# A two-layer correlation convolution on one core: the order in which products fill a PSUM bank, and group statistics one slot ahead

## The reference

```python
def _gn(v, G=32, eps=1e-05):                       # over 16 channels x 1024 pixels
    m, s = mean(g), var(g)
    return (g - m) / sqrt(s + eps)

def conv(feature, conv_w, conv_b):                 # K = 5, per batch
    fn = feature / maximum(norm over channels, 1e-12)
    fp = pad(fn, 2 pixels on each side)
    corr = stack([sum over channels of fp[:, :, r:h + r, cc:w + cc] * fn
                  for cc in range(5) for r in range(5)])
    cat = concatenate([feature, corr], axis=1)     # 512 + 25 channels
    return relu(einsum('oc,bchw->bohw', conv_w, cat) + conv_b)

x = x + conv(_gn(x), w0, b0)
x = x + conv(_gn(x), w1, b1)
```

## Time and profile before

| | |
|---|---|
| median of three runs | 539.26 us (538.2 to 539.94) |
| the profiled execution | 537.76 us, of which the span of all instructions is 536.0 us |
| busy share of the span | PE 88%, DVE 69%, ACT 53%, POOL 24% |
| chain that ended last, by engine | PE 54%, DVE 21%, ACT 8%, issue 6%, DMA 6% |
| channel matmuls (L565) | 1536, 518.6 us of overlapping busy time |
| products (L489, L502) | 4096 matmuls, 171.2 us of overlapping busy time |
| ACT tiles: L655, L662 | 64 of 1526 ns, 52 of 1315 ns |

### The profile page before, as it was taken

The page is one execution under the profiler, slowest core; times in us unless marked ns, Lnnn a source line. Parts: engine busy times, 40 slices in busy tenths (PEclk is TensorE's granted clock), DMA queues, the critical chain, the costliest instruction groups (busy, mean ns, idle before and its releaser), DMA issues.

```text
span 536.0 us, 13926 instructions
## 1 busy us (share of the span) xinstructions
PE 471.2 (88%) x5896; PEld 260.5 (49%) x5896; DVE 370.6 (69%) x869; ACT 285.5 (53%) x338; POOL 126.1 (24%) x179
## 2 busy tenths in 40 slices
PE   0548499499968999999899899999999999999996
PEld 0535255264634646464545546464646454454442
DVE  6789796769778396876859495877868694723322
ACT  1542355566393574839375574749393846623222
POOL 3542410131510313131201313131312112140400
PEclk9989799699998999999999999999999999999999
DMA  8261613440400445357474663131222325363432
GB/s 305 98 223 55 206 42 92 130 120 19 111 25 20 101 176 166 92 179 240 159 231 162 183 245 95 45 93 47 71 67 51 80 70 149 106 190 106 128 126 113
DMA packets 35013, 65.88 MB, mean 123 GB/s; under 512 B 12780, under 2 KB 22052, under 8 KB 34950
## 3 DMA queue, kind: packets, MB, share of 16 engines
q1 hardware_dynamic: 25158, 56.07, 31.4%
q0 software_dynamic: 9792, 8.92, 7.4%
HBM read 33.54 MB, written 28.87 MB: 116 GB/s over the span
## 4 chain that ended last, share of the span: by engine, by line
PE 54%; DVE 21%; ACT 8%; issue 6%; DMA 6%; POOL 2%; SPq 2%; DVEq 0%; ACTq 0%
PE conv_ps L565 38%; PE gram_ps L489 6%; DVE stats L779 5%; PE gram_ps L502 4%; DVE operands L826 4%; PE conv_ps L574 4%; ACT v L662 4%; DMA vol<-corr_h 4%; ACT operands L655 3%; DVE xs L909 2%; DVE operands L832 2%; POOL vol L300 1%; PE turn_ps L555 1%; POOL v L429 1%; DVE wmax L881 1%
## 5 line engine op out<-in xcount | busy, mean ns | idle before, releaser
L565 PE MATMUL conv_ps<-operands,wh 128*128 128x512 f16 x1024 | 324.0, 381 | 1.0 <-DVE wl L897 1.0
L565 PE MATMUL conv_ps<-operands,wl 128*128 128x512 f16 x512 | 194.6, 380 | 0.0
L565 PEld LDWEIGHTS conv_ps<-operands,wh 128*128 128x128 f16 x1024 | 101.4, 99 | 120.0 <-issue 1.9
L689 ACT ACTIVATE act_out<-conv_ps,bias,wdown 128x512 f32<-128x512 f32 x128 | 95.8, 770 | 117.8 <-DVE xs L909 66.7
L826 DVE TENSOR_TENSOR operands<-v,operands 128x1024 f16<-128x1024 f32 x64 | 81.8, 1279 | 61.7 <-ACT v L662 55.4
L909 DVE TENSOR_TENSOR xs<-xs,act_out 128x512 f32<-128x512 f32 x128 | 86.2, 685 | 34.2 <-ACT act_out L689 34.1
L655 ACT ACTIVATE operands<-xs,affine 128x1024 f16<-128x1024 f32 x64 | 97.1, 1526 | 20.7 <-DVE affine L819 20.7
L489 PE MATMUL gram_ps<-operands 128*32 128x108 f16 (+1 forms) x2048 | 85.4, 291 | 13.7 <-DVE operands L832 6.6
L489 PEld LDWEIGHTS gram_ps<-operands 128*32 128x32 f16 x2048 | 79.0, 139 | 21.8 <-issue 20.3
L502 PE MATMUL gram_ps<-operands 128*32 128x72 f16 (+1 forms) x2048 | 85.8, 271 | 2.4 <-issue 2.4
L779 DVE BATCH_NORM_STATS2 stats<-xs 128x6 f32<-128x512 f32 x128 | 79.9, 681 | 2.4 <-DMA xs<-in_x_dram 2.4
(11 more groups left out here) (70 smaller groups left out, 220.5 us busy)
## 6 DMA issues: line engine op xcount, KB each, us to landing
xs<-in_x_dram SPq DMA_DIRECT2D x32, 512.0 KB, 6.4
out_dram<-xs SPq DMA_DIRECT2D x32, 512.0 KB, 3.4
band_dram<-band SPq DMA_DIRECT2D x128, 60.0 KB, 2.7
skew<-band_dram SPq DMA_DIRECT2D x32, 222.5 KB, 3.1
vol<-corr_h POOLq DMA_DIRECT2D x48, 50.0 KB, 2.7
rows_dram<-rows SPq DMA_DIRECT2D x32, 65.8 KB
rows_dram<-rows SPq DMA_DIRECT2D x32, 63.3 KB
mirror<-rows_dram POOLq DMA_DIRECT2D x14, 110.9 KB, 2.5
```

The source lines that it names most:

```text
L565: pe.matmul(conv_ps[:, g % 4, :], w[:, l, t, m * P:(m + 1) * P], opnd[:, u % RING, part, t, n * HALF:(n + 1) * HALF], start=(t == 0 and w ...
L689: act.activation(in_rows(act_out[:, g % 2, :]), by_rows(conv_ps[:, g % 4, :]), ACT.Relu, bias=bias[:, l, m:m + 1], scale=wdown[:, l, m:m + ...
```

## The change

- A window of products lies in gram_ps in the order (y x e) in place of (y e x), the order in which the moving pixels pass. ACT's band copy puts it back into (y e x) and so reads PSUM in steps of two values.
- `norm_tile`, `exact_tile` and POOL's exact tiles write in order and read xs alternating between two image rows (x in steps of 4 bytes, the rows 128 bytes apart). Before they read in order and wrote every second value.
- For the units that `early` names (5 to 8 and 12 to 15) statistics, average and scale are moved ahead. In slot k, for unit k + 2: `stats_tile` 0 and 1 at the head of DVE, 2 at j = 3, 3 at j = 4, `stats_done` at j = 5, `average` on PE at j = 6 behind the turn, `deviations` and `unit_affine` at j = 7. In the next slot ACT does tile 0 of that unit ahead of the band copies. The other units (`late`) keep their places.

```diff
+        def in_bands(a):
+            return a.rearrange("p (y x e) -> p y x e", e=TROWS, x=WI)
+        def by_bands(a):
+            return a.rearrange("p (y e x) -> p y x e", e=TROWS, x=WI)
...
+        AVERAGE_AT, AFFINE_AT = 6, 7
+        def early(u):
+            return valid(u) and u > STEADY + 1 and (unit_layer(u) == 1 or unit_batch(u) < XRING)
+        def late(u):
+            return valid(u) and not early(u)
...
-                    pool.tensor_scalar(by_rows(v[:, t % 2, :]), in_rows(xs[:, ring_slot(unit_batch(u)), t, :]),
+                    pool.tensor_scalar(in_bands(v[:, t % 2, :]), by_bands(xs[:, ring_slot(unit_batch(u)), t, :]),
...
-                at = at.rearrange("p (y e x) -> p y x e", x=WCOLS, e=TROWS)
+                at = at.rearrange("p (y x e) -> p y x e", x=WCOLS, e=TROWS)
...
-                    if valid(k + 1):
+                    if late(k + 1):
                         average(k + 1)
...
+                    if j == AVERAGE_AT and early(k + 2):
+                        average(k + 2)
...
-                act.activation(by_rows(opnd[:, u % RING, 0, t, :]), in_rows(xs[:, ring_slot(unit_batch(u)), t, :]),
+                act.activation(in_bands(opnd[:, u % RING, 0, t, :]), by_bands(xs[:, ring_slot(unit_batch(u)), t, :]),
...
-                act.activation(by_rows(v[:, t % 2, :]), in_rows(xs[:, ring_slot(unit_batch(u)), t, :]), ACT.Identity,
+                act.activation(in_bands(v[:, t % 2, :]), by_bands(xs[:, ring_slot(unit_batch(u)), t, :]), ACT.Identity,
...
-                act.activation(band[:, n, :], gram_ps[:, n, 0:PITCH], ACT.Copy).then_inc(band_sb, 1)
+                act.activation(band[:, n, :].rearrange("p (y e x) -> p y e x", e=TROWS, x=WCOLS),
+                               gram_ps[:, n, 0:PITCH].rearrange("p (y x e) -> p y e x", e=TROWS, x=WCOLS),
+                               ACT.Copy).then_inc(band_sb, 1)
...
             for k in range(STEADY, SLOTS):
+                if early(k + 1):
+                    norm_tile(k + 1, 0)
+                    exact_tile(k + 1, 0)
...
+                    if j == AFFINE_AT and early(k + 2):
+                        deviations(k + 2)
...
-                if valid(k + 1):
+                if late(k + 1):
                     unit_affine(k + 1)
+                if early(k + 2):
+                    stats_tile(k + 2, 0)
+                    stats_tile(k + 2, 1)
...
-                        for t in {4: (0, 1), 5: (2,), 6: (3,)}.get(j, ()):
+                        for t in ({3: (2,), 4: (3,)} if early(k + 2) else {4: (0, 1), 5: (2,), 6: (3,)}).get(j, ()):
                             stats_tile(k + 2, t)
-                        if j == 7:
+                        if j == (5 if early(k + 2) else 7):
                             stats_done(k + 2)
+                    if j == AFFINE_AT and early(k + 2):
+                        unit_affine(k + 2)
```

More of the change, by code:

```diff
@@ L746, in _ @@
                     band_out_of_psum(k, 1)
-                    if valid(k + 1):
+                    if late(k + 1):
                         deviations(k + 1)
-                    if valid(k + 1):
                         norm_tile(k + 1, 0)
                         exact_tile(k + 1, 0)
+                    if valid(k + 1):
                         norm_tile(k + 1, 1)
```

## The result

The changed kernel takes 557.34 us (median of 4 runs, 554.95 to 562.25) against 538.73 before; the ratio is 1.037 [1.033, 1.041]. Ratios stand with their 95% interval and can differ a little from the quotient of the two medians (here 1.035). The change is slower by 3.7%, where 9% was forecast. The time lies inside the forecast range of 527 to 604, but by errors in opposite directions: one term was far too dear, and others stood at nothing. The profiled run took 558.75 us, span 557.0, clock 0.938 over the span where it was 0.973.

The account below looks back on a forecast made before the run. PE was taken as the bound, with one us of margin before the turn. Dearer ACT tiles and early averages, less the products' gain, summed to +48 us on the profiled 537.8: 586, or 587 on the median; range 527 to 604.

Parts of the forecast that it names:

- ACT's tiles: Norm and exact tiles on ACT: reading in jumps adds 0.79 us a tile, the contiguous f16 write saves 0.1.
- T: ACT's time per norm or exact tile: 1.285 us before, forecast 1.98, lower end 1.2 if jumps cost nothing.
- t: When ACT's last tile ends in a slot: 19.3 us with next unit early, 24.2 late, at T = 1.98.
- the rival: The faster rival: ACT's read with jumps costs nothing, T = 1.2, and products gain; 530 us, chance 0.39.
- the skew: SP's second skew issue lands late, so DVE's neighbour scaling waits; at T = 1.2 it sets 14.2 us.
- the five slots between early units: Slots 5, 6, 11 to 13: 34.4 us each, +27.6 in all; 29.3 each, +2.3, at T = 1.2.
- start and end: Kernel's start (units 0 to 2) +4 us and end -2 by the products; together -4 at T = 1.2.
- The moved steps: Early average waits for DVE's 8.9 us behind ACT's last tile; such a slot lasts at least t + 15.1 us.
- The products and the clock: PE's products: side-by-side PSUM writes save 1.0 us with a code stall, 2.3 without; granted clock 1.00 in these stretches.
- Slots 7 and 14, 8 and 9: Slots 7 and 14: PE's own work, 27.9 us each, -3.6; slots 8 and 9: 33.0 each, +4.9.
- the likeliest case: ACT pays for its read with jumps, T = 1.98: 587 us, range 566 to 604, chance 0.54.
- the first rival: ACT's read with jumps costs nothing, T = 1.2, and products gain: 530 us, 525 to 540, chance 0.39.

Follow-up runs that it names:

- e_only: Kernel before with only the early statistics, averages and scales moved; windows and ACT's tiles as before: 557.39 us, ratio 1.0356.
- done4: Changed kernel with the early aggregates one place earlier on DVE, ahead of the addition of j = 4: 548.55 us, ratio 1.0213 to the kernel before.
- avg7: Changed kernel with the early average one place later on PE, behind group 6: 531.31 us, ratio 0.9878 to the kernel before.
- p_only: Kernel before with only the new window order in gram_ps and its band copy: 534.54 us, ratio 0.9945.
- p_split: Kernel before with the new window order and band copy, second bank's products behind the first channel group, average between: 555.54 us, ratio 1.0338.

## Why the prediction was wrong, step by step

**ACT's tiles: the mechanism exists, the size was wrong.** The term was +0.79 us a tile, T = 1.98, and with it t = 19.3 and 24.2. Measured: +0.14 us on the f32 tile, T = 1.36. A price taken from another engine (DVE, two operands, jumps of 80 bytes) was made the forecast for want of a nearer row; the kernel had a nearer hint, that ACT wrote in 8-byte steps at 1.30 ns an element, and I gave it only to the rival. On the f32 tile the sign agrees with the rule on SBUF's lines in the Trainium skill (SBUF — State Buffer, "Specifications (TRN2)"), by which each crossing to a new line pays: 1315 to 1458 ns, 11%, net of what the new write order does. The f16 tile went the other way, from 1526 to 1461 ns.

Three slips in the sum are small: 513 - 362 ns over 200 elements is 0.755 ns and not 0.77; t at T = 1.2 is 13.1 and not 14.0, which the skew's 14.2 hides; slots 3 and 4 at T = 1.2 add up to 65.4 and not 66.4. And the old PSUM step was 20 values, a window's row in the code (`WCOLS`, of which 18 are filled), and not 18.

Put T = 1.36 into the prediction's own sums (t = 14.4 and 19.3): the five slots between early units 29.5, slot 10 34.4, slots 8 and 9 at 28.4, slots 3 and 4 66.9, start and end at -2: 534 us for the profiled run. The measured one is 558.75. So without this error the forecast would have been 0.7% faster, of the wrong sign, and off by 25 us. What follows is about these 25.

**The moved steps: the chain was right, its list of waits was short by one.** For slot 10 the 8.9 us from ACT's end to the average came out to the tenth, and slots 11 to 13 have 8.9 to 9.0. The step "this behind low_tile 3, which waits for ACT's last tile" left something out: three additions were counted in DVE's chain by their duration, 0.6 us each, but the third belongs to the next unit's group 0, whose volume PE holds back to the place right before the turn. The rows of before could show it: `HOLD` in the code, and ACT's rectifications that wait for PE at this place. In slots 4, 5, 6, 11 and 13 this addition is what releases the average (e_only has it too, done4 moves it, avg7 covers it). Its worth is small, though: in slots 5 and 6 the average starts 9.2 us behind ACT's end, only in slot 4 much later, 11.3. And a wait like the measured 1.67 us stands in the prediction's own sums at T = 1.36: 29.5 for a slot less 27.9 of PE's own work is 1.6.

That the five slots between early units took 155.6 us and not 5 x 29.5 has other reasons, which the prediction had at nothing. In slots 5 and 6 ACT's last tile ends at 17.1 and 16.5 and not at 14.4, behind products with code waits of 2.69 and 2.16 us and a clock of half behind them: ACT's tiles share its program with rectifications that wait for PE. In slots 11 and 12 the clock falls behind the wait at the average, and from the average to the slot's end it takes 7.6 us where 6.1 were allowed and 5.95 are taken at full clock (slots 5, 6 and 13).

**The products and the clock: pace right, net gain wrong, clock taken as 1.00.** The step fell to 80 ns as forecast. The forecast kept 1.0 us of a product with a code wait and 2.3 of one without, 21 us in all; p_only measured some 3. I had let the waits grow, but by 1.3 us, and had nothing for the clock: the granted clock of 1.00 in the rows of before was carried over. It fell behind some of the waits and took another 1.5 to 1.7 us each time. By the lost shares above that is up to 20 us more than before, an estimate from the mean clock and the largest part of the 25 that the sum lacks. The Trainium skill's floor of 25 ns between matmul starts (TensorE: Matmul & The Clock Gate, "Wait — 56ns, not 53.3ns?") is contradicted further over four column tiles: eight starts in 80 ns.

**Slots 7 and 14, 8 and 9.** 27.9 us forecast for slot 7, 27.88 measured; slot 14 lost 1.7 to the clock (0.94). Slots 8 and 9 were forecast at 33.0 and came at 28.4 and 29.4; the first is the rival's 28.4, as T would have it, the second has a clock of 0.94.

**The rivals and the sign.** The sign was right by luck, for another reason than mine: the likeliest case put its weight on ACT, and the first rival had the tiles nearly right but lacked the code waits, the clock and the gate. The time fell into the gap between the two cases that the wide range spans; the range of the likeliest alone, 566 to 604, missed it. Of the marks set down, "tiles at 1.2 to 1.3 us alone ends the forecast" was the one nearest to what came: 1.46, and in slots 4 to 6, 11 and 13 a wait at the average that ends with neither ACT's tile nor the skew.

## What to carry to other kernels

When a step moves ahead in an in-order program, list for every instruction that now stands in front of it what that one waits for, and on which engine; an addition that costs 0.6 us stood still for up to 0.85 more (slot 4) for data that PE holds back. A step that synchronises engines belongs one block of independent work (here one channel group) behind the earliest point at which it could run. And a dense run of small matmuls that becomes faster may only reach the wait for its code sooner: hold the time of 256 instructions against the 2.2 to 3.2 us that a packet of code took here, spread the run between long matmuls, then follow what becomes the next wait, here the volume behind the band copy, the low tiles and the correlation. A granted clock of 1.00 in a profile belongs to that schedule; a change that adds waits can lose it.

## What the runs showed of the hardware that was not expected

- PE's waits for code grew from 9.0 to 24.6 us a run when the products became faster and nothing else changed (p_only), and went to 4.1 us, 3.6 of them in the two slots without a split, when a channel group stood between the two halves of 128 matmuls (p_split). Each of these waits over 0.3 us ended 1.2 to 1.6 us after a 16 KB packet of PE's instruction queue had landed.
- In slot 6 of the changed kernel the granted clock fell to 0.52 for 3.46 us behind a wait of 2.16 us in mid-product. The length of a wait alone does not tell whether it falls: behind code waits of 1.70 us each it stayed at 1.00 in slot 8 of that kernel and fell in slot 9 (0.94 over the slot), and behind one of 2.25 us it stayed in slot 8 of p_only.
- ACT reading f32 in jumps of 128 bytes and writing f32 side by side takes 1.46 us for 1024 elements, reading side by side and writing in steps of 8 bytes 1.32; POOL 1.92 and 1.70.
